# Cross-attention and quantised FFN on one core: residual stream kept with features on partitions, last layer norm moved behind the FFN product

## Reference

```python
x = x + _L0_xattn_ref(_layernorm(x), ctx, mask, position_bias, ln_weight, w_q, w_k, w_v, w_out)
#   inside: h = rmsnorm(hidden)*w; softmax(q k^T + bias, masked) v; return hidden_states + attn @ w_out.T
x = x + _L0_ffn_ref(_layernorm(x), w_codes, absmax, W_a, W_b)
#   inside: W = NF4_CODE[w_codes] * absmax;  y = x @ W.T + 2 * (x @ W_a @ W_b)
```

## Time and profile before

| | |
|---|---|
| three runs, median (lowest to highest) | 829.47 us (828.86 to 829.69) |
| the profiled execution, its own time | 830.24 us |
| its span, first to last instruction | 828.1 us |
| busy: PE, DVE, ACT, POOL | 99%, 54%, 54%, 65% |
| granted TensorE clock over the span | 1.000 |

### The profile page before, as it was taken

How to read it: one execution, slowest core, us unless ns; L and a number is a source line. 1 busy time by engine, 2 the same in 40 slices (tenths; PEclk the granted TensorE clock), 3 DMA queues, 4 the chain that set the end, 5 groups by cost and what they waited for, 6 DMA issues and landing times.

```text
span 828.1 us, 15838 instructions
## 1 busy us (share of the span) xinstructions
PE 820.7 (99%) x4730; PEld 721.5 (87%) x4730; DVE 449.4 (54%) x761; ACT 446.7 (54%) x1301; POOL 536.9 (65%) x556
## 2 busy tenths in 40 slices
PE   8999999999999999999999999999999999999998
PEld 7888888988899888988889888998889888898887
DVE  6976544355634656245553555346562455626683
ACT  6856564464726555364644647356553546437632
POOL 1587777467875768756685578757687567865440
PEclk9999999999999999999999999999999999999999
DMA  9403322122211323123231222113230232311102
GB/s 312 136 17 101 112 80 67 55 92 67 94 36 59 98 68 97 25 70 97 75 96 54 90 68 92 38 54 97 69 97 25 70 97 68 107 42 46 47 18 89
DMA packets 50917, 64.59 MB, mean 78 GB/s; under 512 B 10864, under 2 KB 36848, under 8 KB 49872
## 3 DMA queue, kind: packets, MB, share of 16 engines
q1 hardware_dynamic: 50608, 63.81, 25.0%
q10 hardware_dynamic: 288, 0.52, 0.2%
HBM read 44.37 MB, written 4.19 MB: 59 GB/s over the span
## 4 chain that ended last, share of the span: by engine, by line
PE 89%; ACT 4%; SPq 3%; DMA 2%; DVE 2%; issue 1%; ACTq 0%; DVEq 0%
PE w_ps L1235 41%; PE o_ps L1235 35%; PE s_ps L1271 6%; PE s_ps L1277 6%; SPq L352 2%; ACT p_blocks L671 2%; ACT p_blocks L622 1%; DMA wo_raw<-ctx_dram 1%; DMA pT<-p_blocks 1%; PE w_ps L1292 0%; ACT kT L622 0%; PE s_ps L1235 0%; PE w_ps L1334 0%; DVE stats L935 0%; DVE p L1026 0%
## 5 line engine op out<-in xcount | busy, mean ns | idle before, releaser
L550 POOL TENSOR_SCALAR picked<-codes 128x256 f32<-128x256 int32 x112 | 126.3, 1128 | 19.2 <-POOL level L553 15.6
L515 POOL TENSOR_TENSOR p<-pos_raw,mask_add 128x1024 f32<-128x1024 f32 x32 | 69.9, 2185 | 104.5 <-ACT p_blocks L671 104.0
L671 ACT ACTIVATE p_blocks<-p,neg_max 128x128 f32<-128x128 f32 x248 | 96.1, 389 | 51.6 <-DVE neg_max L1028 43.0
L553 POOL TENSOR_TENSOR level<-level,picked 128x256 f32<-128x256 f32 x112 | 88.7, 792 | 20.8 <-POOL picked L550 20.8
L487 POOL TENSOR_TENSOR ring_lo<-k_raw,ring_hi 128x256 fp32r<-128x256 f32 x105 | 76.5, 741 | 27.4 <-ACT ring_hi L622 24.5
L622 ACT ACTIVATE ring_hi<-k_raw 128x256 fp32r<-128x256 f32 x105 | 38.7, 412 | 103.0 <-POOL k_raw L477 103.0
L1051 DVE TENSOR_TENSOR resid<-o_ps,resid 128x512 f32<-128x512 f32 x102 | 68.6, 685 | 43.3 <-PE o_ps L1235 43.1
L1235 PE MATMUL w_ps<-ctx_hi,ring_hi 128*128 128x512 f32 x210 | 84.7, 403 | 0.5 <-ACT kT L622 0.5
L1235 PE MATMUL w_ps<-ctx_hi,ring_lo 128*128 128x512 f32 x210 | 82.0, 391 | 0.0
L1235 PE MATMUL w_ps<-ctx_lo,ring_hi 128*128 128x512 f32 x210 | 81.7, 389 | 0.0
L622 ACT ACTIVATE p_blocks<-p_blocks,row_scale 128x128 f32<-128x128 f32 x248 | 77.0, 390 | 0.0
(11 more groups left out here) (235 smaller groups left out, 2295.2 us busy)
## 6 DMA issues: line engine op xcount, KB each, us to landing
pT<-p_blocks SPq DMA_DIRECT2D x480, 32.0 KB, 1.8
wv_raw<-wv_dram SPq DMA_DIRECT2D x8, 1024.0 KB, 4.8
q_raw<-q_dram SPq DMA_DIRECT2D x32, 256.0 KB, 3.3
wo_raw<-wo_dram SPq DMA_DIRECT2D x32, 256.0 KB, 3.9
k_raw<-k_dram SPq DMA_DIRECT2D x15, 512.0 KB, 3.5
resid<-x_dram SPq DMA_DIRECT2D x2, 1024.0 KB, 10.9
pos_raw<-pos_dram SPq DMA_DIRECT2D x32, 64.0 KB, 3.8
out_dram<-resid SPq DMA_DIRECT2D x7, 256.0 KB, 2.0
```

Source lines behind the costliest of these rows:

```text
L515: pool.tensor_tensor(p[:, :, :], pos, mask_add[:, :, :], ALU.add).then_inc(bias_done, 1)
L550: then(pool.tensor_scalar((level if code == 0 else picked)[:, :], codes[:, :], float(code), NF4[code], match, ALU.mult))
L553: then(pool.tensor_tensor(level[:, :], level[:, :], picked[:, :], ALU.add))
L671: e = act.activation(out(b), p[:, b, :].rearrange("p (k c) -> p k c", c=Q), ACT.Exp, bias=neg_max[:, b:b + 1], accum_out=prob_sum[:, b:b + 1])
```

## The change

The residual stream is stored with features on partitions, `resid[feature, chunk c, token]`. A second copy of x, already turned on the host (`xt_dram`), is loaded into it after the first copy has been used. It is multiplied by 1+r along the tokens: the row of 1024 factors goes from `ln_scale` to DRAM and back, broadcast to all partitions, into `wo_raw`. The term -mr is left out here and added per token at the end. The four multiplications `residual(c)` are tensor-tensor products of 128x1024 on DVE: one between head 0's row scales, one behind them, two ahead of `split_q(2)`. The first two loads of output weights now stand behind the four multiplications.

The output projection swaps its operands, so that its tiles come out with features on partitions; instruction count and shape stay the same. The FFN is applied to the stream without normalising it first. Its weights are centred over the input features: POOL adds the four weight chunks (`ffn_sum`), PE multiplies the sum with a matrix of 1/512 (plain fp32, 128x512), and DVE subtracts the result from each chunk. Then ACT and POOL split them. The token's reciprocal deviation is applied behind the product. Each tile is turned back to tokens (`turn_back`, directly ahead of its own product), ACT adds -mr while it copies it to `v`, DVE makes the statistics from there, POOL the reciprocal deviation, and DVE makes product * r + v, which SP stores.

```diff
-            for hf in range(2):
-                sp.dma_start(resid[:, hf * HB:(hf + 1) * HB, :],
+                sp.dma_start(x_tokens[:, hf * HB:(hf + 1) * HB, :],
...
+            sp.wait_ge(factors_done, 1)
+            sp.dma_start(scale_d.rearrange("(b l) -> l b", b=B), ln_scale[:, :],
+                         allow_slow_non_contiguous=True).then_inc(scale_moved, 16)
+
+            sp.wait_ge(staged, B)
+            for i in range(2):
+                sp.dma_start(resid[:, 2 * i:2 * i + 2, :], xt_d[:, 2 * i:2 * i + 2, :]).then_inc(xt_loaded[i], 16)
+
+            sp.wait_ge(scale_moved, 16)
             sp.wait_ge(ctx_lo_done, 5)
-            load_wo(0, 0)
-            load_wo(1, 1)
+            sp.dma_start(scale_row, scale_d.partition_broadcast(P)).then_inc(scale_moved, 16)
...
             load_pos(2, 0)
+
+            sp.wait_ge(hidden_done, C)
+            load_wo(0, 0)
+            load_wo(1, 1)
...
+            pool.tensor_tensor(ffn_sum, wv_raw[:, 0, :], wv_raw[:, 1, :], ALU.add).then_inc(ffn_sums, 1)
...
+            for c in range(C):
+                pool.wait_ge(ffn_hi_done, c + 1)
+                lo(ffn_weights(ctx_lo, c), wv_raw[:, c, :], ffn_weights(ctx_hi, c)).then_inc(ffn_lo_done, 1)
...
+            def residual(c):
+
+                dve.wait_ge(xt_loaded[c // 2], 16)
+                dve.wait_ge(scale_moved, 32)
+                dve.tensor_tensor(resid[:, c, :], resid[:, c, :], scale_row, ALU.mult).then_inc(hidden_done, 1)
...
             xn_low(1)
-            for b in range(HB):
-                residual(b)
             split_first(6, ctx_lo[:, 2, :, :], ctx_sum[1], ctx_hi[:, 2, :, :])
...
             scale_rows(0, 0)
-            residual(HB)
+            residual(0)
             scale_rows(0, 1)
-            for b in range(HB + 1, B):
-                residual(b)
+            residual(1)
...
             dve.sem_inc(p_turned_done, 2)
+            residual(2)
+            residual(3)
             split_q(2)
...
+            for t in range(B):
+                add_pair(PAIRS - 1, t, tile_ps[t % 4])
+                if 1 <= t <= C:
+                    centre_ffn(t - 1)
+                if t > C:
+                    stream_low(t - C - 1)
...
+                for i, at in enumerate([slice(0, D)] if b < B - 1 else [slice(0, D // 2), slice(D // 2, D)]):
+                    dve.wait_ge(out_done, B * PAIRS + b + 1 + i)
+                    dve.scalar_tensor_tensor(v[:, b, at], tile_ps[(b + i) % 4][:, 0:at.stop - at.start], rstd[:, b:b + 1],
+                                             v[:, b, at], ALU.mult, ALU.add).then_inc(out_added, 1)
+                if b + 1 < B:
+                    last_stats(b + 1)
...
+                output(t, last_wo_hi, last_wo_lo, tile_ps[t % 4])
+                if t == 1:
+
+                    pe.wait_ge(mean_of_done, 1)
+                    pe.wait_ge(ffn_sums, C - 1)
+                    pe.matmul(w_ps[0][:, :], mean_of, ffn_sum, start=True, stop=True).then_inc(ffn_mean_done, 1)
...
             for b in range(B):
-                if b + 1 < B:
-                    if b + 1 >= 2:
-                        pe.wait_ge(xT_lo_done, b)
-                    ffn_transpose(b + 1)
-                if b == 0:
+                if b:
+
+                    if b == 1:
+                        pe.wait_ge(ffn_centred, C)
+                    turn_back(b)
+                else:
                     pe.wait_ge(ffn_lo_done, C)
                 ffn_product(b)
```

More of the change, by code:

```diff
@@ L176, in xattn_ffn @@
         x_stage = [wv_raw[:, i, :] for i in range(4)] + two_tiles(flat_blocks(pT[:, :, :, :])) + [v[:, b, :] for b in (4, 5)]
-        ffn_stage = [kT[:, i, f * D:(f + 1) * D] for i in range(2) for f in range(2)]
+        x_tokens = flat(resid[:, :, :]).rearrange("p (b d) -> p b d", b=B)
+        scale_row = flat(wo_raw[:, :, :])
+        ffn_sum = flat(k_raw[:, 0:2, :])
+        mean_of = absmax[:, 0:P]
         mask_raw = codes[:, :].bitcast(u8).rearrange("p (b k) -> p b k", b=B)
@@ L232, in xattn_ffn @@
         x_loaded = [sem(f"x_loaded{i}") for i in range(2)]
+        xt_loaded = [sem(f"xt_loaded{i}") for i in range(2)]
+        scale_moved = sem("scale_moved")
         mask_loaded = sem("mask_loaded")
@@ L830, in odd_head @@
                     split_wo(i, 2 * g + j // 2 + 1, wo_hi)
-                if last:
-                    act.wait_ge(ffn_loaded, 16)
-                    act.wait_ge(keys_done, PRODUCTS * m + 2)
-                    for c in range(C - 1):
-                        split_ffn(c)
                 drain_q(h + 1, 1, query_bank(j, 1))
@@ L901, in _, with stream_high, shift @@
                 attention(2 * (H - 2) + 2 * hf + 1, 1, hf, s_flat(hf))
-            act.wait_ge(last_ffn_loaded, 16)
-            split_ffn(C - 1)
-            def ffn_norm(b):
-                act.wait_ge(norm_done, 2 + b + 1)
-                if b >= 4:
-                    act.wait_ge(ffn_turned, b - 4 + 1)
-                act.activation(ffn_stage[b % 4], resid[:, b, :], ACT.Identity, bias=ln_shift[:, b:b + 1],
-                               scale=rstd[:, b:b + 1]).then_inc(ffn_staged, 1)
-            ffn_norm(0)
-            ffn_norm(1)
-            for b in range(B):
-                if b in range(2, B - 1):
-                    ffn_norm(b + 1)
-                act.wait_ge(ffn_turned, b + 1)
-                copy(xn_hi[:, :, b * L:(b + 1) * L],
-                     w_ps[b % 2][:, :].rearrange("p (c t) -> p c t", c=C)).then_inc(xT_hi_done, 1)
-                if b == 1:
-                    ffn_norm(2)
+            act.wait_ge(keys_done, PRODUCTS * PAIRS)
+            for c in range(C):
+                split_ffn(c)
+            def stream_high(b):
+                act.wait_ge(out_added, B * (PAIRS - 1) + HB * (b // HB + 1))
+                at = slice(b * L, (b + 1) * L)
+                copy(xn_hi[:, :, at], resid[:, :, at]).then_inc(xT_hi_done, 1)
+            def shift(b):
+                act.wait_ge(returned, b + 1)
+                act.activation(v[:, b, :], w_ps[(b + 1) % 2][:, :], ACT.Identity, bias=ln_shift[:, b:b + 1]).then_inc(shifted, 1)
+            act.wait_ge(queries_done, 2 * H)
+            act.wait_ge(attn_done, 2 * H)
+            stream_high(0)
+            shift(0)
+            for b in range(1, HB + 1):
+                stream_high(b)
+            for b in range(1, B):
+                shift(b)
+                if b + HB < B:
+                    stream_high(b + HB)
         @block.vector
@@ L1148, in odd_head @@
                     split_wo(i, h - 1 + i, wo_hi, wo_lo)
-                if last:
-                    for c in range(2):
-                        split_ffn(c)
                 split_q(h + 2)
```

158 lines of the change are left out of this document (73 added, 85 removed).

## The result

The changed kernel takes 832.13 us (median of 10 runs, 830.55 to 833.24), the kernel before, run beside it, 829.64 us (10 runs, 828.86 to 830.49). The ratio is 1.0027, with a 95% interval of 1.0019 to 1.0035: 2.5 us slower, by the ratio 2.2 (1.6 to 2.9). The profiled execution took 832.54 us with a span of 830.7, 2.6 us over the span before. Its time is only 2.3 us over that of the profiled execution before (830.24), since less of it lies outside the span: 1.8 us and not 2.1. That holds in every execution of the changed kernel and of the kernels made from it (1.8), against 2.1 in those of the kernel before; no run tells why. Three places account for 2.1 of the 2.6 us in the span: the start of head 1, the product for the means, and the layer norm behind the last turn.

The account below looks back on a forecast made before the run. PE, busy 820.7 of 828.1 us, was taken as the bound. Mean product 0.89, tail 0.2 and head 1 1.35 sum to 2.44 us, added to the median 829.47 for 831.9 us; range 830.3 to 833.5.

Parts of the forecast that it names:

- Mean product, 0.89: Last output projection: the added plain fp32 128x512 product costs its whole length on a full PE, 0.89 us (0.45 to 1.0).
- The lower bound: Mean product: two instructions at the fp32r pace, 0.45 us in all, if loading weights and not columns bounds short products.
- Behind the last product, 0.2: Kernel's end: batch 7's layer norm after its turn delays the last addition from T+2.90 to T+3.1, 0.2 us (0 to 0.5).
- Head 1, 1.35: Start of head 1: POOL's late key sum delays ACT's query copy, for which PE waits, 1.35 us (0 to 2.6).
- one multiplication in the gap 1.22: Start of head 1: one DVE multiplication between POOL's low half and key sum adds 1.22 us; key sum ends 60.76.
- as all of head 1's chain moves with it: Head 1: the whole chain shifts with the late query copy, so the 0.5 us wait behind it stays as is.
- the 0.33 of the forecast: Start of head 1: about 0.33 us of key sum lateness are free before ACT's query copy is delayed.
- Nothing for the updates taken out, the transfers, the later loads: Head 0 and SP's queue: removed updates gain nothing; the factor row, turned x and later output-weight loads cost 0.
- The cover of the row of factors: SP, ahead of DVE's first multiplication: to DRAM at most 7.2 us, broadcast issued 37.7, at least 9.7 us before use; hidden.
- FFN weights, 0: Before the first FFN product: centring and splitting the weights is covered by 0.3 to 0.9 us, cost 0.
- POOL keeps its pace: Rival at head 1: key sum not late, head 1 costs 0 to 0.5 us; 830.1 to 831.1 us, chance 0.25.
- Both multiplications ahead of POOL: Rival at head 1: both multiplications get in before the key sum, 1.22 us more, 833.1 us; chance 0.1.

Follow-up runs that it names:

- the fp32r mean: Changed kernel with both operands of the mean product rounded to fp32r, one instruction and not two: 830.67 us, 1.0015 of the kernel before.
- four products: Changed kernel with the plain fp32 mean product issued four times into the same bank: 834.18 us, 1.0056 of the kernel before.
- turn 7 early: Changed kernel with batch 7 turned back one product earlier, behind the turn of batch 6: 831.22 us, 1.0024 of the kernel before.
- the same with fp32r: Changed kernel with batch 7 turned back one product earlier and the mean product in fp32r: 830.90 us, 1.0018 of the kernel before.
- with its statistics: Changed kernel with batch 7 turned back one product earlier and its DVE statistics ahead of product 6's scaling and adding: 830.68 us, 1.0014 of the kernel before.
- the late multiplications altered: Five changed kernels: two late multiplications left out (830.84 us), fed from PSUM (830.45), placed apart (832.72), apart with mean and tail edits (831.94), PSUM with those edits (829.58).
- the three terms out: Changed kernel with fp32r mean, batch 7's turn and statistics early, and late multiplications taking one operand from PSUM: 829.58 us, 1.0001 of the kernel before.

## Why the prediction was right, point by point

The forecast of 831.9 us (measured 832.13) came true, and so did its three places: a full PE pays for the product, the last layer norm stands behind the last turn, and DVE and POOL take turns at the start of head 1. One of the three terms was too large, and the way in which it reaches PE was another. That the number came within 0.2 us is in part luck: the terms measured 2.07 us and not 2.44, a further 0.5 of the span fell elsewhere, most of it in the stretch that scatters, and 0.3 us were given back outside the span, which the forecast had taken as unchanged.

**Mean product, 0.89.** Measured 0.86, and 0.90 with the gap behind it. The columns decide, as assumed: nearly four times the 128-column pace (0.22 a product). The lower bound, the fp32r pace, is what the kernel with rounded operands shows (0.23), and that is one instruction where plain fp32 is two. The Trainium skill (FP8 and Floating Point Precision, "TensorE Precision Notes") has four passes for true fp32, from which the prediction's estimate of 0.91 came; the trace comes near it, 0.86 being 3.7 times 0.23.

**Behind the last product, 0.2.** Measured 0.20, with the last addition at T+3.04 (forecast T+3.1). The shift took 0.70 as taken. The share of the longer scalar-tensor-tensor instruction, 0.06, was not in the forecast's account.

**Head 1, 1.35.** Measured 0.97 in the first trace; this term was mis-sized. The place, the wait of PE for the query copy behind the key sum, and the order low half, one multiplication, key sum were as forecast; POOL's bias ended at 57.86 (forecast 58.05). But the step "one multiplication in the gap 1.22" was wrong. The multiplication started at 57.88, during POOL's low half of 57.82 to 58.56, and POOL's next sum was held not by the multiplication's whole length but by 0.75 us (1.49 less 0.74). So the key sum ended at 60.23 instead of 60.76, and the copy behind it was 0.83 late instead of 1.37; PE's wait was 0.55 us, not about 1.3.

The step "as all of head 1's chain moves with it" was wrong as well. Head 1's bias on DVE followed the query copy only in part: it started at 62.37, 0.34 us late, since `split_q(2)`, no longer held by POOL, took 0.73 and not 1.21. What made head 1 late was another path, not in the forecast: both multiplications and `split_q(2)` held POOL, and its last sum, 2.40 us late, held ACT's two copies of key weights and the exponentials behind them. The old slack on that path, 1.33 us, was four times the 0.33 of the forecast, and so the two accounts come to prices that are not far apart.

The cost also has two values. Seven traces have this code unaltered. In three (the two of the changed kernel and the fp32r mean) head 1 costs 0.97 to 0.98; in four (four products, turn 7 early, the same with fp32r, and with its statistics) 0.62 to 0.64. What differs is who comes first at `residual(0)`, ten microseconds earlier. In the changed kernel, DVE and POOL in order of time:

```profile
50.57 1.23 DVE L1011 TENSOR_TENSOR resid<-resid,wo_raw 128x1024 f32<-128x1024 f32 x1
...
50.57 1.81 POOL L579 TENSOR_TENSOR level<-level,picked 128x256 f32<-128x256 f32 x1 [0.18 <-POOL picked L576]
```

And in the kernel with turn 7 and its statistics early:

```profile
50.48 1.81 DVE L1011 TENSOR_TENSOR resid<-resid,wo_raw 128x1024 f32<-128x1024 f32 x1
...
50.47 0.74 POOL L579 TENSOR_TENSOR level<-level,picked 128x256 f32<-128x256 f32 x1 [0.18 <-POOL picked L576]
```

The two start within 0.01 us of each other, and one of them has to wait: POOL in the first, DVE in the second. In the second POOL's bias ends 2.10 us ahead of head 1's scores instead of 1.76, and PE's wait at head 1 is 0.21 instead of 0.55. All three traces with the higher cost have the first outcome and all four with the lower one the second, as have the five of the kernels with the late multiplications altered; no run forces the one or the other. The forecast took a single end of POOL's bias (58.05); it is a race with two outcomes, both inside its bounds of 0 to 2.6.

**Nothing for the updates taken out, the transfers, the later loads.** Confirmed: no wait of PE names them, and with the three terms out the time is that of before within the interval. The cover of the row of factors was thinner than forecast, though: its way to DRAM took 9.0 us and not at most 7.2, so the broadcast was issued at 39.23 and not at 37.7; it landed 9.2 us later, at 48.4, only 2.1 us ahead of the first use at 50.57. The two loads of turned x landed 14.8 us after their issue at 30.67, long before.

**FFN weights, 0.** Confirmed. POOL's last low half ended at 801.39; taken back by the 1.43 us that everything there is later, that is 799.96 (forecast 799.9). DVE's first stream half ended at 801.94 and the product started at 802.58: covered by 0.6 us (forecast 0.3 to 0.9).

**Rivals.** *POOL keeps its pace* falls by name: its sums doubled. With the lesser of the two outcomes of the race, though, the cost of head 1 comes within 0.15 us of that rival's upper bound for it. *Both multiplications ahead of POOL* did not come for the first key sum in any trace, as the two engines alternated; for the last sum, which sets the price, both were ahead.

## What to carry to other kernels

Before an element-wise instruction with two SBUF operands is moved to a place where VectorE is idle, read what GpSimd runs there and who waits for each of its next results: each engine holds up the other, and the chain behind the held engine that ends last sets the price, which need not be the one with the new wait in it. An operand in PSUM took the contention away here. Where a wait of TensorE was there before and is still there behind the new one, follow the old one back first. When a chain behind the last product is to be shortened, look for its steps in every queue, since moving the first step alone leaves the next one behind whatever it was queued on.

## What the runs showed of the hardware beyond that

- The Trainium skill (GPSIMD Engine Reference, "1. Specifications") has POOL's SBUF interfaces shared with VectorE; the trace agrees, and the runs give the size. In every row read here the instruction that came second waited for the other's end, whichever engine it was on: POOL's 128x256 sum went from 0.74 to 1.49 us beside a two-operand VectorE multiplication of 128x1024; the same multiplication went from 1.21 to 1.71 on average beside the sums, to 1.81 beside a decoding step and to 3.17 beside a bias addition of 2.85. With one operand in PSUM (four of 128x512 in 2.48 us) POOL stayed at 0.74.
- A plain fp32 product of 128x512 is two instructions of 0.43 us, in fp32r one of 0.23.
- ACT's copy of 128x512 out of PSUM with a bias operand took 0.70 us, between 0.60 for the plain one and 0.82 for one out of SBUF with two pointer operands.
